# A graph network's adjacency matrices: built from one-hots of the source's low seven bits and of a combined key, instead of one-hots of the whole source and of the destination

## What is computed

```python
src = jnp.concatenate([_s, _d, _loop]); dst = jnp.concatenate([_d, _s, _loop])
_o = jnp.argsort(dst, stable=True); src = src[_o]; dst = dst[_o]
# layer 0 (and five times in layer 2)
neigh = segment_sum(h1[src], dst, num_segments=1536)
# layer 1, twice: one sum for each of two edge types
msg = where((edge_type == 0)[:, None], msgs[0], msgs[1]); agg = segment_sum(msg, row, 1536)
# layer 3: weighted
out = segment_sum(support[src] * edge_vals[:, None], dst, 1536) + bias
```

## Time and profile before

| what | value |
|---|---|
| median of three runs | 2180.89 us |
| the profiled execution's own time | 2184.54 us |
| its span, first to last instruction | 2182.7 us |
| build stage, first to last one-hot | 29.9 to 460.3 us |
| PE busy over the whole span | 1992.7 us (91%) |
| DVE busy over the whole span | 906.3 us (42%) |
| one-hots of the source (L585) | 384 instructions, 241.1 us |
| one-hots of the destination (L586) | 384 instructions, 166.1 us |
| window matmuls (L1124) | 4608 instructions, 235.5 us |

### The profile page before, as it was taken

One profiled execution on the slowest core, in us unless ns is written; L12 is line 12 of the kernel. 1 busy time (PEld: TensorE's weight loads), 2 busy tenths in 40 slices (PEclk: granted clock), 3 DMA queues, 4 the chain that ended last, 5 costly groups with the idle time before them and its releaser, 6 DMA issues.

```text
span 2182.7 us, 33277 instructions
## 1 busy us (share of the span) xinstructions
PE 1992.7 (91%) x11904; PEld 1024.8 (47%) x11905; DVE 906.3 (42%) x1802; ACT 668.5 (31%) x1276; POOL 168.0 (8%) x214
## 2 busy tenths in 40 slices
PE   4878787858999989999999999999999999987998
PEld 3656565645333344544445444444444444443443
DVE  6969696941411126211111222344343434376032
ACT  1545454541476404111111100023231323266100
POOL 2424242410000000000000000000000000000000
PEclk9999998977999997999999999999999999998999
DMA  4767676856010014110000111350000000012011
GB/s 110 183 172 185 172 185 158 194 165 260 1 34 1 1 53 153 55 39 1 1 20 0 39 39 39 118 210 6 20 4 21 1 17 9 15 44 73 10 49 48
DMA packets 47438, 158.33 MB, mean 73 GB/s; under 512 B 9316, under 2 KB 11260, under 8 KB 38816
## 3 DMA queue, kind: packets, MB, share of 16 engines
q1 hardware_dynamic: 42880, 142.28, 22.6%
q10 hardware_dynamic: 4384, 13.78, 1.8%
HBM read 120.38 MB, written 35.65 MB: 71 GB/s over the span
## 4 chain that ended last, share of the span: by engine, by line
PE 80%; DVE 7%; issue 5%; DVEq 3%; ACT 3%; DMA 1%; SPq 0%; POOL 0%; ACTq 0%; POOLq 0%
PE psum L1176 27%; PE psum L1190 27%; PE psum L1399 6%; PE psum L1124 5%; PE psum L1250 2%; PE psum L1303 2%; DVE hs L586 2%; DVE hs L585 2%; PE psum L1350 2%; PE psum L1090 2%; PE psum L1172 2%; PE psum L1163 1%; DVEq L585 1%; ACT adj L879 1%; DVEq L586 1%
## 5 line engine op out<-in xcount | busy, mean ns | idle before, releaser
L1190 PE MATMUL psum<-hs,adj 128*128 128x512 f16 x2880 | 643.1, 380 | 0.8 <-DVE hs L690 0.8
L1176 PE MATMUL psum<-wb,xt 128*128 128x512 f32 x1152 | 521.1, 608 | 15.1 <-DVE hs L818 13.4
L1190 PEld LDWEIGHTS psum<-hs,adj 128*128 128x128 f16 x2880 | 280.0, 98 | 358.8 <-issue 45.2
L1176 PEld LDWEIGHTS psum<-wb,xt 128*128 128x128 f32 x1152 | 219.7, 195 | 278.0 <-issue 275.9
L585 DVE TENSOR_SCALAR hs<-hs 128x1536 f16<-128x1536 f16 x384 | 241.1, 628 | 82.5 <-PE psum L1124 50.7
L1124 PE MATMUL psum<-hs 128*128 128x96 bf16 x4608 | 235.5, 211 | 22.9 <-DVE hs L586 19.0
L1124 PEld LDWEIGHTS psum<-hs 128*128 128x128 f16 x4608 | 210.8, 100 | 38.5 <-DVE hs L586 28.7
L586 DVE SCALAR_TENSOR_TENSOR hs<-hs 128x96 bf16 x384 | 166.1, 433 | 0.0
L964 ACT ACTIVATE adj<-hs,pbias 128x512 f32<-128x512 f32 x216 | 134.5, 707 | 85.2 <-PE psum L1250 85.2
L997 ACT ACTIVATE ua<-ua 128x512 f32<-128x512 f32 x60 | 37.8, 631 | 350.7 <-DVE ua L832 198.0
L769 DVE TENSOR_TENSOR vt<-psum,adj 128x512 f32<-128x512 f32 x24 | 16.6, 692 | 278.4 <-PE psum L1176 278.4
(11 more groups left out here) (207 smaller groups left out, 1668.9 us busy)
## 6 DMA issues: line engine op xcount, KB each, us to landing
hs<-in_L_gnn_basis SPq DMA_DIRECT2D x64, 960.0 KB, 7.5
aw_scratch<-xt ACTq DMA_DIRECT2D x12, 768.0 KB, 4.4
adj<-aw_scratch SPq DMA_DIRECT2D x1, 9216.0 KB, 38.2
x_scratch<-adj SPq DMA_DIRECT2D x24, 256.0 KB, 2.1
hs<-x_scratch SPq DMA_DIRECT2D x24, 256.0 KB, 2.6
ts_scratch<-adj SPq DMA_DIRECT2D x1, 4608.0 KB, 17.6
as_scratch<-adj SPq DMA_DIRECT2D x1, 4608.0 KB, 28.9
adj<-ts_scratch SPq DMA_DIRECT2D x1, 4608.0 KB, 13.3
```

The costliest lines, as they stand in the source:

```text
L1176: x = pe.matmul(psum[:, bank, :], xt[:, i, k, :], w[:, k, :], start=first and k == 0, stop=last and k == 3)
L1190: x = pe.matmul(psum[:, i % 2 + (4 * half if own else 0), :], adj[:, m, j, P * i:P * i + P], hs[:, t, half, j, :], start=n == 1 or (own an ...
```

## The change

The source number is split. Its low seven bits (0 to 127) make one one-hot of 128 columns, `onehot_s`, which now is the weights of every matmul of the tile. The other bits (the source block j, 0 to 11) go into a key together with the destination d and the type t. `onehot_t` has the 384 columns of 24 d + 12 t + j for the window's 16 destinations; `onehot_w` and `onehot_l` have the 192 columns of 12 d + j. `onehot_w` is written as f32: its 32 bits hold two bf16 weight parts side by side (the pair), which two matmuls read apart; `onehot_l` is the third weight part in bf16. So a tile has four one-hots and four matmuls. A step is three tiles and not four, and three windows share PSUM in turns instead of two.

To compare in f16, keys are made relative to a group of four windows. POOL subtracts the group's offset from all keys ahead of time (`krel`, two buffers). A is no longer summed by PE: ACT copies only the typed part and the weighted part, and POOL adds the two types of a whole block, 128 x 1536, into `adj`. The hardware loop over passes is gone; all 96 windows and all 64 chunks are written out, and turn lots are spread in the same way behind every block but the last.

```diff
-STEP = 4
+STEP = 3
 MOST = -(-ET // STEP)
-NPART = 6
+TW = W * 2 * NT
+AWW = W * NT
+REL = 4
+RING = 3
...
-        wrem = lay(2 * EC, F32, "p (a t) -> p a t", a=2)
-        vals = lay(EC * NPART, BF16, "p (t v) -> p t v", v=NPART)
-        iota_s = lay(N, F16)
-        onehot_s = lay(STEP * N, F16, "p (k s) -> p k s", k=STEP)
-        onehot_d = lay(STEP * NPART * W, BF16, "p (k v w) -> p k v w", k=STEP, v=NPART)
+        wpair = lay(EC, F32)
+        wpair16 = wpair.bitcast(BF16).rearrange("p (t h) -> p h t", h=2)
+        wlast = lay(EC, F32)
+        krel = lay(2 * 2 * EC, F32, "p (b a t) -> p b a t", b=2, a=2)
+        iota_s = lay(REL * TW, F16)
+        onehot_s = lay(STEP * P, F16, "p (k s) -> p k s", k=STEP)
+        onehot_t = lay(STEP * TW, F16, "p (k c) -> p k c", k=STEP)
+        onehot_w = lay(STEP * AWW, F32, "p (k c) -> p k c", k=STEP)
+        onehot_w16 = onehot_w.rearrange("p k c -> p (k c)").bitcast(BF16).rearrange("p (k c h) -> p k h c", k=STEP, h=2)
+        onehot_l = lay(STEP * AWW, BF16, "p (k c) -> p k c", k=STEP)
...
-        win = [psum[:, 3 * b:3 * b + 3, :].rearrange("p k c -> p (k c)").rearrange("p (j c) -> p j c", j=NT)
-               for b in range(2)]
+        def evicted(w):
+
+            return win_free[w % RING], w // RING + 2
...
+        win = [psum[:, 2 * b:2 * b + 2, :] for b in range(RING)]
...
-            with sp.Fori(0, NB - 1) as g:
-                chunks(g, True)
-            chunks(NB - 1, False)
+            for n in range(CH):
+                l, c = n // (CH // 2), n % (CH // 2)
+                lot = lot_of[("basis", l, c)]
+                if n + 2 < CH:
+                    sp.wait_ge(side_ps, lot + 1)
+                    load_chunk(n + 2)
...
-            with pool.Fori(0, NB) as g:
-                for u in range(GB):
-                    b, s = u % 2, u // 8
-                    if u % 8 == 0:
-
-                        pool.wait_ge(side_ps, stage_free_at(g, s))
-                    pool.wait_ge(win_free[b], HB * g + u // 2 + 2)
-                    part = [wparts[:, b, :, W * v:W * v + W] for v in range(3)]
-                    pool.tensor_tensor(wsum[:, b, :, :], part[0], part[1], ALU.add).then_inc(wsum_ready[b], 1)
-                    pool.wait_ge(wsum_ready[b], HB * g + u // 2 + 1)
-                    pool.tensor_tensor(aw_stage[:, s % 2, :, W * (u % 8):W * (u % 8) + W],
-                                       wsum[:, b, :, :], part[2], ALU.add).then_inc(wparts_free[b], 1)
+            pool.wait_ge(keys_ready, 1)
+            for a in range(2):
+                x = pool.tensor_copy(krel[:, 0, a, :], ecol[:, 1 + a, :])
+            x.then_inc(krel_ready, 1)
+            for n in range(NW // REL):
+
+                if n + 1 < NW // REL:
+                    pool.wait_ge(krel_ready, n + 1)
+                    if n:
+                        for k in range(1, RING + 1):
+                            pool.wait_ge(*evicted(REL * n - k))
+                    pool.tensor_scalar(krel[:, (n + 1) % 2, 0, :], krel[:, n % 2, 0, :], float(-REL * TW), None, ALU.add)
+                    pool.tensor_scalar(krel[:, (n + 1) % 2, 1, :], krel[:, n % 2, 1, :], float(-REL * AWW), None, ALU.add).then_inc(krel_ready, 1)
+                if n % 2:
+                    s = n // 2
+                    for k in range(RING):
+                        pool.wait_ge(*evicted(PER * s + PER - 1 - k))
+                    pool.tensor_tensor(adj[:, 0, :, P * s:P * s + P], typed[:, s % 2, 0, :, :], typed[:, s % 2, 1, :, :], ALU.add).then_inc(typed_summed, 1)
...
-            dve.tensor_copy(erow[0:ER, 0:3, :], erow_i[0:ER, 0:3, :]).then_inc(erow_ready, 1)
-            dve.wait_ge(erow_ready, 1)
-            dst2 = erow[0:ER, 1, :].rearrange("p (h e) -> p h e", h=2)
+            dve.tensor_scalar(erow_i[0:ER, 3, :], erow_i[0:ER, 0, :], P - 1, None, ALU.bitwise_and)
+            dve.tensor_copy(erow_d[0:ER, :], erow_i[0:ER, 1, :])
+            step(dve.tensor_scalar(erow_i[0:ER, 0, :], erow_i[0:ER, 0, :], 7, None, ALU.logical_shift_right))
+            dve.tensor_copy(erow[0:ER, 0, :], erow_i[0:ER, 3, :])
+            dve.tensor_scalar(erow[0:ER, 1, :], erow_i[0:ER, 2, :], 0.0, float(NT), ALU.not_equal, ALU.mult)
+            step(dve.tensor_copy(erow[0:ER, 2, :], erow_i[0:ER, 0, :]))
+            step(dve.tensor_tensor(erow[0:ER, 1, :], erow[0:ER, 1, :], erow[0:ER, 2, :], ALU.add))
+            dve.scalar_tensor_tensor(erow[0:ER, 1, :], erow_d[0:ER, :], float(2 * NT), erow[0:ER, 1, :], ALU.mult, ALU.add)
+            dve.scalar_tensor_tensor(erow[0:ER, 2, :], erow_d[0:ER, :], float(NT), erow[0:ER, 2, :], ALU.mult, ALU.add).then_inc(erow_ready, 1)
...
-            dve.memset(vals[:, :, 0:1], 1.0)
-            dve.tensor_scalar(vals[:, 0:EC, 1], ecol[:, 2, :], 0.0, None, ALU.is_equal)
-            dve.tensor_scalar(vals[:, 0:EC, 2], ecol[:, 2, :], 0.0, None, ALU.not_equal)
-            step(dve.tensor_copy(vals[:, 0:EC, 3], ecol[:, 3, :]))
-            step(dve.tensor_tensor(wrem[:, 0, :], ecol[:, 3, :], vals[:, 0:EC, 3], ALU.subtract))
-            step(dve.tensor_copy(vals[:, 0:EC, 4], wrem[:, 0, :]))
-            step(dve.tensor_tensor(vals[:, 0:EC, 5], wrem[:, 0, :], vals[:, 0:EC, 4], ALU.subtract))
+            x.then_inc(keys_ready, 1)
+            dve.wait_ge(keys_ready, 1)
+            step(dve.tensor_copy(wpair16[:, 1, :], ecol[:, 3, :]))
+            step(dve.tensor_tensor(wlast, ecol[:, 3, :], wpair16[:, 1, :], ALU.subtract))
+            step(dve.tensor_copy(wpair16[:, 0, :], wlast))
+            step(dve.tensor_tensor(wlast, wlast, wpair16[:, 0, :], ALU.subtract))
...
-            with dve.Fori(0, NB) as g:
-                following = window(g * GB)
-                for u in range(GB):
-                    w = g * GB + u
-                    first, steps, before = unpack(following)
-                    if u + 1 < GB:
-                        following = window(w + 1)
-                    with dve.Fori(0, steps) as q:
-                        for k in range(STEP):
-                            t = nc.s_assert_within(first + STEP * q + k, 0, EC - 1, skip_runtime_bounds_check_because="a window's steps end less than a step past its last tile")
-                            dve.wait_ge(onehot_free[k], before + q + 1)
-                            dve.tensor_scalar(onehot_s[:, k, :], iota_s, ecol[:, 0, bass.ds(t, 1)], None, ALU.is_equal)
-                            dve.scalar_tensor_tensor(
-                                onehot_d[:, k, :, :], iota_s[:, bass.ds(w * W, W)].unsqueeze(1).broadcast_to([P, NPART, W]),
-                                ecol[:, 1, bass.ds(t, 1)], vals[:, bass.ds(t, 1), :].rearrange("p o v -> p (o v)").unsqueeze(2).broadcast_to([P, NPART, W]),
-                                ALU.is_equal, ALU.mult).then_inc(onehot_ready[k], 1)
+                return dve.value_load(wrow_i[0:1, 0, w:w + 1], min_val=0, max_val=PACKED)
+
+            following = window(0)
+            for w in range(NW):
+                first, steps, before = unpack(following)
+                if w + 1 < NW:
+                    following = window(w + 1)
+                n, u = w // REL, w % REL
+                if u == 0:
+                    dve.wait_ge(krel_ready, n + 1)
+                with dve.Fori(0, steps) as q:
+                    for k in range(STEP):
+                        t = nc.s_assert_within(first + STEP * q + k, 0, EC - 1, skip_runtime_bounds_check_because="a window's steps end less than a step past its last tile")
+                        dve.wait_ge(onehot_free[k], before + q + 1)
+                        dve.tensor_scalar(onehot_s[:, k, :], iota_s[:, 0:P], ecol[:, 0, bass.ds(t, 1)], None, ALU.is_equal)
+                        dve.tensor_scalar(onehot_t[:, k, :], iota_s[:, TW * u:TW * u + TW], krel[:, n % 2, 0, bass.ds(t, 1)], None, ALU.is_equal)
+                        for pairs, weight in ((onehot_w, wpair), (onehot_l, wlast)):
+                            x = dve.tensor_scalar(pairs[:, k, :], iota_s[:, AWW * u:AWW * u + AWW], krel[:, n % 2, 1, bass.ds(t, 1)],
+                                                  weight[:, bass.ds(t, 1)], ALU.is_equal, ALU.mult)
+                        x.then_inc(onehot_ready[k], 1)
...
-                    act.activation(adj[:, 0, :, bass.ds(w * W, W)], win[b][:, :, 0:W], ACT.Copy)
-                    if u % 8 == 0:
-                        act.wait_ge(side_ps, stage_free_at(g, s))
-                    act.activation(typed[:, s % 2, :, :, W * (u % 8):W * (u % 8) + W].rearrange("p m j d -> p j m d"),
-                                   win[b][:, :, W:3 * W].rearrange("p j (m d) -> p j m d", m=2), ACT.Copy)
-                    act.wait_ge(wparts_free[b], HB * g + u // 2 + 1)
-                    act.activation(wparts[:, b, :, :], win[b][:, :, 3 * W:6 * W], ACT.Copy).then_inc(win_free[b], 1)
+                if u == 0 and s >= 2:
+                    act.wait_ge(side_ps, staged_again(s))
+                    act.wait_ge(typed_summed, s - 1)
```

(14 more changed lines are left out.)

156 lines of the change are left out of this document (65 added, 91 removed).

## The result

The changed kernel is slower: 2208.8 us (four runs, 2206.5 to 2211.2) against 2183.1 beside it on the same chip, a ratio of 1.0127 with an interval of 1.0108 to 1.0147. The forecast was 2114 us, the range 2078 to 2150.

What follows compares the result with a forecast made beforehand. DVE was taken to bound the build: 293 (tiles) + 58 (POOL) + 12 (PE) = 363 us against 430.4, 67 us less, so 2114 us against the median 2180.9; range 2078 to 2150 us.

Steps and rivals of the forecast that it cites:

- ACT and the waits added: ACT's window copies in the build: strided stores, even at twice the time, stay under 206 us of 430; cost nothing.
- PE: Build matmuls: 0.47 us a tile, 263 us in all, well below DVE; DVE's waits for PE 12 us, bounds 0 and 39.
- the ten second steps: New jumps back in the build, each nothing to 9 us; nothing taken in sum, up to three (28 us) in the range.
- Number of tiles: Build with steps of three tiles: 106 steps, 318 tiles instead of 384.
- DVE per tile: DVE's four one-hots in the build: 241, 308, 368 and 318 ns, 0.92 us a tile with overlap, 293 us for 318.
- POOL: POOL's hold on DVE in the build: additions 42 us, key subtractions 16, together 58 us; bounds 17 and 84.
- The loop over passes: The build's hardware loop: its three ends go, saving 39 us at most, of which 28 us are "issue".
- Prologue and end: Around the build: source split adds some 2.6 us, removed work gives back 1.2, two POOL additions 1.2; net nothing.
- The loads: Rival: basis chunk loads with two buffers bound the build, 32 pairs taking 387 us, time 2139 us; chance 0.20.
- The slower rival: Rival: DVE's four short instructions do not overlap their starts, 1.24 us a tile, build 464 us, time 2214 us; chance 0.06.
- The waits did not vanish: Rival: DVE's waits for PE vanish in the build, DVE needs 310 us, loads bind, time 2083 us; chance 0.18.
- a granted clock of 1.00: Sign: granted clock 1.00 through the whole build, without the 0.66 at a pass's end.

Runs made afterwards that it cites:

- e1: The changed kernel with both ACT window copies reading PSUM with a stride and storing in line: 2165.1 us, 0.993 of the kernel before.
- e2: The kernel before with its typed copy alone storing with a stride, as in the changed kernel: 2222.3 us, ratio 1.0212.
- e12: e6 with ACT's two copies storing with a stride again, as in the changed kernel: 2165.0 us, 0.9931 of the kernel before.
- e4: The changed kernel with 27 extra ACT copies of 192 PSUM columns behind window 0, in 13 forms; only durations read, e.g. f16 384 ns at 4 bytes.
- e6: e5 with six one-hot buffers of each kind instead of three: 2115.9 us, 0.9713 of the kernel before.
- e5: e1 with step numbers taken from a list of this input, so without inner loops and loads of counts: 2146.1 us, 0.9856 of the kernel before.
- e10: e6 with three buffers for the basis chunks instead of two: 2090.7 us, 0.9583 of the kernel before.
- e11: e6 with POOL's 12 additions of 1536 columns cut to two columns, leaving out the unweighted adjacency: 2089.8 us, 0.9577 of the kernel before.
- e3: The kernel before with its four passes written out as one, all 96 windows: 2137.4 us, 0.9813 of the kernel before.

## Why the prediction was wrong, step by step

**The step that failed is "ACT and the waits added".** It said: "even at twice the time they stay under the 206 us of 430 that ACT has now". The typed copy took 3.9 times as long, not twice, and the two copies of a window 2.2 us from start to end instead of 0.7 (e1). The second fault is worse: I weighed ACT by its sum. With 285 of 456 us ACT never was the busiest, yet its copies stand in a chain (window copies, side copies, PE's bank, PE's next tiles, DVE's buffers), and there their length counts in each turn window. e1 gives 44 us for it, e2 43 in the old scheme, e12 49. No trace of before showed a strided store, so it was a price to be bounded, and "twice" had no row behind it; the Trainium skill's sentence on lines of 16 bytes, cited at e4, spoke against this change, and I did not weigh it.

**"PE": waits of DVE for PE, 12 us, bounds 0 and 39.** Mis-sized: 89 in the changed kernel, 41 in e1, just above the bound even without the slow copies. I had named the cause (three tiles ahead instead of four) and then set it against PE's gain of 0.45 us a tile. e6 prices three buffers against six at 30 us; four buffers were not tried. PE's own time was right only at full clock, 0.42 us a tile for 0.47. 84 of the 318 tiles ran at the lower of TensorE's two levels and took twice that. The second longest of DVE's waits for PE shows both, at a granted clock of 0.53 from 228.4 to 232.0 us:

```profile
228.40 1.78 PE L1095 MATMUL psum<-hs,attw 120*32 120x512 f32 x8 [2.29 <-ACT adj L886]
...
230.94 0.53 PE L1126 MATMUL psum<-hs 128*128 128x384 f16 x1
...
231.56 0.25 DVE L591 TENSOR_SCALAR hs<-hs 128x128 f16<-128x128 f16 x1 [5.18 <-PE psum L1128]
...
231.74 0.48 PE L1126 MATMUL psum<-hs 128*128 128x384 f16 x1
```

PE waited 2.29 us for ACT, then its basis lot took 1.78 us instead of 1.07, and a tile 0.80 instead of 0.42 (230.94 to 231.74).

**A term that was missing: issue gaps at window starts.** I wrote that no row of DVE within a pass waits for "issue" over 0.2 us, and kept the ten second steps only. The changed kernel has 53 gaps with 29.9 us, all at a window's first tile, none over 2.1 us. No second step cost the 9 us that the range allowed for. e5 gives 16 to 19 us back. That the last instruction of a tile, now 0.32 us, is too short to cover the next window's register work, which the 0.61 us one covered, is my reading; e5 shows only that the gaps go with loops and loads.

**Right, and shown.** *Number of tiles*: 318. *DVE per tile*: 0.248, 0.313, and in e10 0.372 and 0.322 us by median, against 0.241, 0.308, 0.368, 0.318, and 0.92 from one to the next; e10's build of 339 us is 293 and what follows:

```profile
58.60 3.08 POOL L482 TENSOR_TENSOR adj<-wb 128x1536 f16<-128x1536 f16 x1 [11.67 <-ACT xt L909]
58.65 3.54 DVE L594 TENSOR_SCALAR hs<-hs 128x192 f32<-128x192 f16 x2
```

*POOL*: an addition is 3.1 us for 3.5, and two DVE instructions of 0.61 us together take 3.54 beside it, an exclusive lock as the Trainium skill (SBUF — State Buffer, two separate sides) has it; e11 measures 38.5 us for the 42 I took. The key subtractions take 0.78 and 0.73 us, above my bound of 0.59, but cost less than the 16 us I took: DVE's instructions beside them lie 11 us in sum above their medians in e10, 8 in e11. In all some 42 us, not 58. *The loop over passes*: 42 us (e3) for 39; no wait of 9 us is left. One row was misread there: the DMA share of 0.84 is that of 150 to 175 us; while DVE stood still (126.9 to 135.9 us) it was 0.54, and 0.39 in the piece from 130 to 135 us, so the 9 us are not the price under a busy queue. *Prologue and end*: the first one-hot starts at 29.4 for 29.9 us and the layers take the same time.

**The sum again.** From 2183: passes -42, slow copies +44, issue gaps +19, three buffers (against six) +30, POOL and the rest -25: 2209. Each term was measured with the ones before it already mended, and holds what the granted clock changed along with it. The last term is what is left over; e6, in which copies, gaps and buffers are mended, lies 21 under e3. The forecast had the passes in full, the waits that the buffers bring at 12, the copies at nothing and the gaps not at all.

**The rivals.** The loads don't bind the changed kernel (3.3 us of waits), but they are next in line: 17 us in e1, 57 in e6, and a third buffer then gives 25 us. The slower rival (starts don't overlap) is wrong as a mechanism, though its 2214 us lies near the result: that is luck. The waits did not vanish but grew, DVE's idle time from 82 to 119 us; only e10, with 6 us left, comes near that rival's 2083. I expected a granted clock of 1.00; it was not. Two stretches of the changed kernel, then e3's build (after the stretch: busy time and count of PE, PEld, DVE, ACT, POOL, then granted clock, DMA share, GB/s):

```profile
100.00:200.00 100.00, 73.87 (x523) 39.17 (x521) 70.10 (x270) 61.87 (x73) 12.39 (x11) 0.80 0.61 150
200.00:300.00 100.00, 70.13 (x533) 35.28 (x534) 75.68 (x280) 66.74 (x79) 18.69 (x15) 0.90 0.72 178
```

```profile
29.00:420.00 391.00, 327.34 (x5804) 249.65 (x5804) 354.90 (x768) 202.66 (x430) 154.40 (x191) 1.00 0.78 192
```

L1095 takes 754 ns on average instead of 606, and the basis lots 86.6 us instead of 68.4. With the slow tiles (84 x 0.38 = 32 us) that is an estimated 50 us more of PE's time. How much of it is in DVE's 89 us of waits no run separates, and part of the 44 us may be this, since e1 also raised the granted clock of the build from 0.87 to 0.90. e10, at 0.93 with its basis matmuls at 639 ns and 6 us of idle DVE, shows that a kernel bound by DVE hardly feels it. What sets the clock was not tried.

## What to carry to other kernels

A busy sum clears an engine of nothing when it sits between two others with shallow buffers: follow one window through all engines and add up the chain. Price a layout change by the byte step of its stores, and let the read side (here PSUM) take the stride. Count buffers in microseconds: three tiles of 0.92 us are 2.8 us, and in e1 PE is away for 2.4 to 3.2 us, mostly 2.8, when two turn lots and a basis lot stand together, before the 0.4 us of its next tile; the step size and the number of buffers should be two constants, not one.
